# Cross-attention: VectorE adds the last two tiles of partial sums, and the products of ones run over one tile in place of two for 25 steps

## What is computed

```python
scores = jnp.einsum('bhqd,bhkd->bhqk', q, k) * scale + bias[None]
attn = jax.nn.softmax(scores, axis=-1)
out = jnp.einsum('bhqk,bhkd->bhqd', attn, v)
```

## Time and profile before

| | |
|---|---|
| median of three runs | 1706.61 us |
| the profiled execution | 1706.23 us |
| its span | 1704.6 us |
| granted TensorE clock, mean | 0.988 |
| TensorE busy | 1644.8 us, 96%, 10889 matmuls |
| weight loads busy | 1327.7 us, 78% |
| VectorE busy | 1066.9 us, 63% |
| ScalarE busy | 752.6 us, 44% |
| GpSimd busy | 751.9 us, 44% |

### The profile page before, as it was taken

One profiled execution on the slowest core, in us unless ns is written; L12 is line 12 of the kernel. 1 busy time (PEld: TensorE's weight loads), 2 busy tenths in 40 slices (PEclk: granted clock), 3 DMA queues, 4 the chain that ended last, 5 costly groups with the idle time before them and its releaser, 6 DMA issues. The chain is left out here.

```text
span 1704.6 us, 34503 instructions
## 1 busy us (share of the span) xinstructions
PE 1644.8 (96%) x10889; PEld 1327.7 (78%) x10889; DVE 1066.9 (63%) x1892; ACT 752.6 (44%) x1364; POOL 751.9 (44%) x848
## 2 busy tenths in 40 slices
PE   9998999999999998899999998899999999999997
PEld 8887787788787776777787776678888888888876
DVE  6554566565656555877978987754564646436653
ACT  4334344434434425666656665523342424224442
POOL 3201333332333315888887856442451514215451
PEclk9999999999999998999999999899999999999999
DMA  8657666667667649977778775347655546456774
GB/s 247 220 208 217 180 197 181 186 199 207 183 187 196 167 132 186 196 189 178 163 166 191 168 175 174 111 103 258 189 160 162 184 137 214 105 148 201 235 256 108
DMA packets 192257, 309.52 MB, mean 182 GB/s; under 512 B 22248, under 2 KB 143800, under 8 KB 184192
## 3 DMA queue, kind: packets, MB, share of 16 engines
q1 hardware_dynamic: 172624, 227.16, 48.3%
q0 software_dynamic: 14768, 46.27, 11.3%
q10 hardware_dynamic: 4752, 34.61, 5.5%
HBM read 224.30 MB, written 83.66 MB: 181 GB/s over the span
## 5 line engine op out<-in xcount | busy, mean ns | idle before, releaser
L2302 DVE TENSOR_REDUCE part_max<-a_s_bank 112x1 f32<-112x500 f32 (+1 forms) x368 | 225.2, 671 | 50.8 <-PE a_s_bank L1987 35.2
L2188 ACT ACTIVATE a_prob<-a_st_bank 125x448 f32<-125x448 f32 x384 | 189.8, 545 | 146.5 <-PE a_st_bank L2010 138.2
L3043 DVE TENSOR_TENSOR e_u_sb<-o_or_u_bank,e_b_row 128x512 f32<-128x512 f32 x134 | 92.4, 689 | 224.1 <-PE o_or_u_bank L2780 218.2
L2778 PE MATMUL o_or_u_bank<-e_w_hi,e_xT_hi 128*128 128x512 f32 x520 | 207.2, 398 | 1.0 <-DVE e_w_lo L3036 0.4
L2780 PE MATMUL o_or_u_bank<-e_w_hi,e_xT_lo 128*128 128x512 f32 x520 | 204.5, 393 | 0.0
L2779 PE MATMUL o_or_u_bank<-e_w_lo,e_xT_hi 128*128 128x512 f32 x520 | 203.9, 392 | 0.0
L2860 ACT ACTIVATE e_g_hi<-e_g_bank 128x256 fp32r<-128x256 f32 x133 | 51.2, 385 | 340.2 <-PE e_g_bank L2787 337.5
L2960 POOL DMA_INDIRECT out<-l_rows,e_y_row x33 | 53.2, 1613 | 286.8 <-DVE l_rows L3086 144.5
L1828 POOL TENSOR_TENSOR a_part_sum<-a_prob 125x448 f32<-125x448 f32 x128 | 146.5, 1149 | 24.4 <-ACT a_prob L2188 24.2
L1044 POOL TENSOR_TENSOR m_prob_sum<-m_prob 112x224 f32<-112x224 f32 x128 | 93.9, 738 | 137.9 <-ACT m_prob L1286 130.0
L2936 POOL TENSOR_TENSOR e_w_lo<-e_w_raw,e_w_hi 128x1024 fp32r<-128x1024 f32 x28 | 102.5, 3671 | 49.6 <-ACT e_w_hi L2870 49.6
(11 more groups left out here) (451 smaller groups left out, 4304.6 us busy)
## 6 DMA issues: line engine op xcount, KB each, us to landing
e_w_raw<-L_ffn_Wl SPq DMA_DIRECT2D x96, 512.0 KB, 10.6
e_b_row<-L_ffn_bl ACTq DMA_DIRECT2D x33, 1024.0 KB
m_c_in<-ctx POOLq DMA_DIRECT2D x12, 1000.0 KB, 6.4
v<-m_cv SPq DMA_DIRECT2D x48, 224.0 KB
a_v_sb<-v SPq DMA_DIRECT2D x32, 336.0 KB
m_q_st<-q SPq DMA_DIRECT2D x93, 112.0 KB, 3.0
m_k_st<-k SPq DMA_DIRECT2D x93, 112.0 KB, 3.1
first<-k SPq DMA_DIRECT2D x24, 375.0 KB, 5.6
```

What stands on the lines that cost most here:

```text
L2188: act.activation(prob[s % 2][:, hh, 2 * u:2 * u + 2, :], st_bank[n % SB][0:CR, 0:2 * S].rearrange("p (e q) -> p e q", e=2), ACT.Exp).then_ ...
L2302: dve.tensor_reduce(out, scores, AX.X, ALU.max).then_inc(s_free, 1)
L2778: pe.matmul(out, xT_hi[:, slot, k, :], w_h, start=(k == 0), stop=False)
```

## The change

A new semaphore and a new VectorE operation, `whole_sum(s)`: for s < 25, when all partial sums of step s are there, VectorE adds the second remaining tile of all four heads to the first (125 x 896 elements in, in place, both inputs in SBUF). It stands in VectorE's loop step s behind the maxima of head 1. TensorE, for these steps, waits for it in place of `sum_done`, and multiplies the ones by one tile in place of two. Steps 25 to 31 stay as they are.

```diff
+        whole_ready = c.sem("a_whole_ready")
...
-                    pe.wait_ge(sum_done, sums_before(s + 1))
+                    if s < STORING:
+                        pe.wait_ge(whole_ready, s + 1)
+                    else:
+                        pe.wait_ge(sum_done, sums_before(s + 1))
                     if s == 0:
                         pe.wait_ge(const_ready, 1)
-                    tiles = [(part_sum, 0), (part_sum, 1)] if s < STORING else [(prob, 4), (prob, 5), (part_sum, 0), (part_sum, 1)]
+                    tiles = [(part_sum, 0)] if s < STORING else [(prob, 4), (prob, 5), (part_sum, 0), (part_sum, 1)]
...
+                def whole_sum(s):
+                    w = s % 2
+                    dve.wait_ge(sum_done, sums_before(s + 1))
+                    dve.tensor_tensor(part_sum[w][:, :, 0, :], part_sum[w][:, :, 0, :], part_sum[w][:, :, 1, :], ALU.add).then_inc(whole_ready, 1)
+
...
                         if first_step(s) is not None:
                             maxima(first_step(s), hh)
+                        if 0 <= s < STORING and hh == 1:
+                            whole_sum(s)
```

## The result

Six runs of the changed kernel have their median at 1726.24 us (1721.42 to 1730.63), beside 1706.3 us for the kernel before; the ratio is 1.0108, 95% interval 1.0090 to 1.0127. The medians are 19.9 us apart; by the ratio, to which the interval belongs, the change makes the kernel slower by 18.4 us (15.4 to 21.7).

What follows compares the result with a forecast made beforehand. TensorE was taken to set the pace, its bank refills waiting for VectorE's maxima. Delays less gains, summed over the kinds of step, gave +15.9 us: 1706.2 to 1722.1 (1722.5 against the median), range 1706 to 1734.

Steps and rivals of the forecast that it cites:

- The ends: TensorE's products of ones: one tile less gains 0.375 us a step, 9.4 in 25 steps; lost behind a projection.
- The margins: VectorE's maxima against TensorE's bank refills: 0.43 to 0.78 us of added delay that TensorE doesn't feel, by kind of step.
- d: Growth of VectorE's queue per step: 1.6 us (bounds 1.16 and 2.3), of which 0.45 is waiting for GpSimd.
- step 11: Kind s mod 4 = 3: margin 0.65 us, TensorE held up 0.95; four such steps cost 2.3 us net.
- step 12: Kind s mod 4 = 0: margin 0.50 us, TensorE held up 1.10; six such steps cost 4.35 us net.
- step 9: Kind s mod 4 = 1, with output projection: margin 0.43 us, held up 1.17, gain lost; five steps cost 5.85 us.
- step 10: Kind s mod 4 = 2: margin 0.78 us, TensorE held up 0.82; five such steps cost 2.2 us net.
- Steps 0 to 3: First four steps: put at nothing, TensorE's 3.4 us wait for the keys' DMA covering loss and gain; otherwise about 2 us.
- The addition isn't hidden: Answers the rival that VectorE's idle time hides the addition and TensorE keeps all 9.4 us: 1697 us, chance 0.05.
- No port wait: Rival: VectorE's addition never waits for GpSimd, 1.16 us of queue a step; 6.7 us slower, 1713 us, chance 0.17.
- GpSimd as the one that is late: Rival: GpSimd's delayed partial sums hold up VectorE, then TensorE; 1728 us, worst case 1735; chance 0.15 beyond 1729.
- The test in the trace of before: Step 19's routing work behind head 1 against step 11: formula gives TensorE 0.32 us delay, trace shows 0.29.

Runs made afterwards that it cites:

- one_tile: The changed kernel without VectorE's addition, TensorE still over one tile (half of the partial sums not counted): 1702.4 us, ratio 0.9974.
- only3: The change made in steps 19, 20 and 22 alone, other steps as before: 1713.77 us, ratio 1.0039.
- change_again: The unaltered change measured once more in a later run: 1725.14 us beside 1705.74 before, ratio 1.0112.
- reduce: The changed kernel with a one-input SBUF reduction of the same 896 elements in the addition's place: 1719.47 us, ratio 1.0068.
- twice: skip5 with the addition made twice, one behind the other: 1771.26 us, ratio 1.0377.
- late: The change with the addition moved behind the last head's maxima (head 2's in steps with a projection): 1718.0 us, ratio 1.0059.
- late_ten: Addition behind the last head's maxima in steps 1, 2, 6, 7, 10, 11, 14, 15, 18, 23 alone, others as before: 1704.71 us, ratio 0.9994.
- skip5: The change in 20 steps, with steps 3, 19, 20, 21 and 22 left as before: 1715.48 us, ratio 1.0043.
- reduce20: skip5 with the one-input reduction in place of the addition: 1709.28 us beside 1705.74 before, ratio 1.0017.

## Why the prediction was right

The forecast, 1722.1 (1722.5 against the median) in a range of 1706 to 1734, holds the 1726.24 that was measured, and the sign and the mechanism were right. The sum was right for a smaller part than its total suggests.

- **The ends.** The gain is 0.375 us a tile: 0.36 to 0.40 in one_tile. That it is lost behind a projection: 0.01 there.
- **The margins** stand. With the delay d that each step shows (how much later the maximum behind the addition starts within its step), the formula of the prediction gives for step 11: d = 1.56, 1.56 - 0.65 - 0.375 = 0.54, measured 0.52; for step 12: d = 1.00, 1.00 - 0.50 - 0.375 = 0.13, measured 0.12; for step 9: d = 1.27, 1.27 - 0.43 less its own gain of 0.375 = 0.47, measured 0.54; for step 10: 1.00 - 0.78 - 0.375, and the gain of step 9 lost at its start, + 0.375 = 0.22, measured 0.23. (The prediction booked that lost gain to step 9; the sum of the two steps is the same.)
- **The step that failed: d.** It was put at 1.6 us everywhere. The addition takes 1.08 alone and adds 1.00 to the queue, not 1.16: it overlaps with its neighbours as the reductions do. And the wait for GpSimd is 0.17 us on the mean (1.25 less 1.08), not 0.45, which was reckoned as a random arrival. The arrivals aren't random, the regular steps of one kind repeat to 0.03 us: two kinds of step never wait, one waits 0.55, one 0.2. The small operations beside which the 0.45 was chosen are no guide either: they never go ahead of GpSimd, this addition often does (last section). Single steps fall out of this: step 5 waited 0.92, and step 15 of the second profile, behind a stretch at the lower clock, 0.11. For steps 4 to 18 the prediction's terms add up to 11.1 us; 6.2 were measured.
- **The term that was missing: the clock.** The prediction reckoned what TensorE waits and nothing for what follows a wait. Steps 19 to 24 were to cost 4.8 us and cost 10.7 (9.9 in the second profile); only3 shows 8.3 us for three of them, up to 6.9 of which by the granted clock. The 4.9 us too much of the one part and the 5.9 too little of the other cancel; that the total came so near is luck.
- **Steps 0 to 3** were put at nothing. They end 3.3 us later in the one profile of the change and at the same time in the other (716.7 us in both before and change_again); among all kernels run here this point lies between 712.6 and 722.0, with no order by what they change. The trace can't tell more.
- **The rivals.** The addition isn't hidden. "No port wait" is reduce, nearly: 1.0068, 11.6 us, where 6.7 were reckoned; without the clock's part it is 6.6. GpSimd as the one that is late did not come: its last sum of step 9 ends at 789.84 and VectorE comes to the addition at 790.70, 0.86 us of room where there had been 1.36.
- **The test in the trace of before** (step 19 against step 11) was worth making: it confirmed the margins, and they held. The same pair could have shown the danger: step 19 had used up its margin, and a wait added there is a full wait of TensorE.

The signs named ahead: 424 records, right; the mean of the new line, 1.25, just under the 1.3 to 1.7 named; the weight loads' waits from 6.4 to 24.3, right (over 20); steps 8 to 12 longer together, by 62.73 - 61.17 = 1.6 us, less than the 2 to 3 named; GpSimd's additions at about 2.2 us, 15 above 1.9 in the 25 steps, where one or so in each was named.

## What to carry to other kernels

An engine with idle time in sum can still be the wrong place for added work: what counts is the next consumer behind the insertion, and the time between a buffer's release and its refill in the trace tells that to a tenth of a microsecond. Instructions taken from the engine that sets the pace are worth less than their sum wherever it already waits for another engine, here 4.4 of 9.4 us. And a stall of TensorE of more than 1 us can cost more than itself: look for steps in which other work already uses up the margin, for there the stalls add up and the clock falls.

## What the runs showed of the hardware

**Which of VectorE and GpSimd goes first.** The Trainium skill, SBUF — State Buffer, section "Who interferes with whom", has the first to issue keep the other out for its whole instruction. For VectorE's addition of 125x896 it depends on how far GpSimd's addition (1.15 us alone) has come when VectorE's starts. From 0.13 to 0.43 us behind GpSimd's recorded start VectorE went ahead every time (51 cases in eight profiles: 1.08 us for VectorE, 2.2 to 2.5 for GpSimd, as in 829.10 above with 2.34); from 0.60 to 1.0 us GpSimd finished first every time, in 1.13 to 1.17, and VectorE ended about 0.95 us after it (the second additions of twice left aside, which met a GpSimd addition already held up). Between lies a border: at 0.47 to 0.52 GpSimd held it in ten cases, all against its first kind of addition (L1829), and VectorE passed at 0.50 (twice, step 11) and 0.53 (late, step 23), both against its second (L1833). Below 0.11 us both were seen.

It isn't a matter of the start alone: VectorE's small operations on SBUF, of 64 columns or less, never went ahead. Of those that started 0.13 to 0.43 us into a GpSimd addition, 51 TENSOR_TENSOR and 21 CAST in the twelve profiles, all ended just behind it, by up to 0.09 us, and GpSimd kept its 1.15 (the 0.92 at 937.26 in the earlier trace rows is one). The weight split of 512 columns (L2470 before the change) went ahead at 0.17 to 0.33 and lost at 0.46, but went ahead again at 0.54 and 0.55 (three cases). A CAST has a single input, so one input in SBUF doesn't free every operation: of 32 columns it takes 0.17 us alone and took 0.94 when it started 0.25 us into a GpSimd addition (reduce). By the recorded starts, which on GpSimd are rough, the measurement decides against the rule as far as the order goes; if GpSimd takes what the two share only some time after its recorded start, part of it could still hold. That the two exclude one another, and that a reduction with one SBUF input is free of it, the runs bear out. What makes large operations differ from small ones no run here shows.

**The clock after a stand.** Over the twelve profiles, from 680 to 1010 us, the granted clock fell to 1.2 GHz 38 times, and in 37 of them TensorE had just stood for 1.17 us or more. The reverse is less sure. Of 32 stands over 1.8 us 26 were followed by a fall; a stand of 2.02 us (late_ten, step 5) and two of 2.56 us (twice) were not. Of 28 stands of 1.1 to 1.8 us 11 were, and the same stand of 1.50 us in step 14 was followed by a fall in change_again and reduce and by none in the first profile of the change, skip5 and reduce20. Behind a stand below 1.1 us there was none: the regular steps stand up to 0.78 us, and the clock there was 1.00 over 198 us. Nor does a fall always cost time: with the one in step 14 of change_again, 3.4 us long, steps 14 and 15 take 25.95 us together, without it 25.89. What decides between a fall and none no run here separates.
